# Two routers' position tables in 16 bit, weights copied one stage earlier, and a new order in the rotary products and at the end

## What is computed

```
x = x + ga * causal_attention(h)              # layer 0
x = x + gb * one_of_8_experts(h)              # layer 0: a token goes to its best expert, 320 places each
K = rotary(Xn @ Wk); V = rotary(Xn @ Wv)      # layer 1, the mixer
A = sum over tokens of (K/|K|) * (V/|V|)      # one row of 256
A = 0.5*A + 0.5
x = x + ga * ((A * Q) @ W_out + b_out + h)
out = sum over the 2 best experts e of mult[t,e] * ((silu(h @ w1[e].T) * (h @ w3[e].T)) @ w2[e].T)
x = x + gb * out                              # layer 1: 8 experts, inner width 512
```

## Time and profile before

| | us |
|---|---|
| median of 3 runs | 1075.88 (1074.55 to 1075.96) |
| the profiled execution, its own time | 1077.33 |
| the span of the profile | 1075.6 |
| PE busy | 966.8 (90%) |
| DVE busy | 638.4 (59%) |
| ACT busy | 517.6 (48%) |
| POOL busy | 291.8 (27%) |

### The profile page before, as it was taken

One profiled execution on the slowest core, in us unless ns is written; L12 is line 12 of the kernel. 1 busy time (PEld: TensorE's weight loads), 2 busy tenths in 40 slices (PEclk: granted clock), 3 DMA queues, 4 the chain that ended last, 5 costly groups with the idle time before them and its releaser, 6 DMA issues. The chain is left out here.

```text
span 1075.6 us, 24763 instructions
## 1 busy us (share of the span) xinstructions
PE 966.8 (90%) x9950; PEld 637.2 (59%) x9951; DVE 638.4 (59%) x1683; ACT 517.6 (48%) x809; POOL 291.8 (27%) x347
## 2 busy tenths in 40 slices
PE   6788899999999999997769999978885799999993
PEld 4433334455444444444347777766664799999993
DVE  5568999999889979675710010079677533333331
ACT  3532567767875786663221222246533444444440
POOL 2100320110111011132034434224550255544541
PEclk9978999999999999999869999999997899999997
DMA  5881000000000000000944677330560032233224
GB/s 184 177 175 21 2 2 2 3 3 2 3 3 2 2 3 2 2 4 25 377 139 110 201 223 224 94 91 1 177 215 1 26 57 49 46 49 48 46 43 98
DMA packets 63279, 78.87 MB, mean 73 GB/s; under 512 B 12096, under 2 KB 54976, under 8 KB 62736
## 3 DMA queue, kind: packets, MB, share of 16 engines
q1 hardware_dynamic: 50688, 61.54, 19.0%
q0 software_dynamic: 11968, 15.47, 8.6%
q10 hardware_dynamic: 528, 0.52, 0.1%
HBM read 58.12 MB, written 21.36 MB: 74 GB/s over the span
## 5 line engine op out<-in xcount | busy, mean ns | idle before, releaser
L622 ACT ACTIVATE k_prob<-f_s 128x1024 f32<-128x1024 f32 (+3 forms) x320 | 270.1, 896 | 121.3 <-PE f_s L460 120.6
L682 DVE TENSOR_REDUCE k_mpart<-f_r 128x1 f32<-128x512 f32 x384 | 250.5, 685 | 34.3 <-PE f_r L403 32.0
L403 PE MATMUL f_r<-k_ks,k_qs 112*32 112x512 bf16 (+3 forms) x2560 | 212.7, 357 | 19.7 <-DMA k_qs<-q_dram 7.8
L460 PE MATMUL f_s<-k_qs,k_ks 114*32 114x512 bf16 (+3 forms) x2560 | 175.4, 350 | 1.9 <-ACT k_prob L622 1.3
L882 POOL TENSOR_SCALAR_AFFINE_SELECT k_prob<-k_prob 128x256 f32<-128x256 f32 x128 | 51.3, 407 | 383.9 <-ACT k_prob L622 382.6
L403 PEld LDWEIGHTS f_r<-k_ks,k_qs 112*32 112x32 bf16 x2560 | 71.0, 96 | 136.6 <-DVE k_mpart L682 56.0
L476 PE MATMUL f_o<-k_prob,k_vaug 128*32 128x512 f32 (+3 forms) x1280 | 147.0, 531 | 1.5 <-POOL k_prob L882 1.4
L679 DVE CUSTOM_DVE_ANT_0 k_unread<-f_r,k_causal 128x128 bf16<-128x128 f32 (+3 forms) x256 | 121.1, 484 | 19.2 <-PE f_r L403 18.1
L460 PEld LDWEIGHTS f_s<-k_qs,k_ks 114*32 114x32 bf16 x2560 | 66.1, 97 | 77.7 <-issue 27.6
L2347 DVE TENSOR_TENSOR mid<-silu_g,e_u 128x512 f32<-128x512 f32 x39 | 26.8, 687 | 111.3 <-PE e_u L2248 110.4
L1419 DVE SCALAR_TENSOR_TENSOR outr<-p_o,k_w,k_mod 128x256 f32<-128x256 f32 x16 | 7.7, 484 | 128.2 <-PE p_o L1348 128.2
(11 more groups left out here) (401 smaller groups left out, 1263.4 us busy)
## 6 DMA issues: line engine op xcount, KB each, us to landing
k_w1T<-in_L_ffn_w_dram SPq DMA_DIRECT2D x18, 512.0 KB, 9.7
k_w1T<-in_L_ffn_wi_dram SPq DMA_DIRECT2D x8, 1024.0 KB, 5.9
k_w1T<-in_L_ffn_wo_dram SPq DMA_DIRECT2D x8, 1024.0 KB, 9.5
k_qs<-q_dram SPq DMA_DIRECT2D x6, 768.0 KB, 9.5
h_rows<-k_h SPq DMA_DIRECT2D x8, 512.0 KB, 6.5
sum<-k_x SPq DMA_DIRECT2D x8, 512.0 KB, 6.2
q_dram<-k_room SPq DMA_DIRECT2D x12, 256.0 KB, 8.8
k_rot_t<-in_L_ffn_w_dram SPq DMA_DIRECT2D x6, 512.0 KB, 4.7
```

Of the source, the lines that this page charges most:

```text
L403: last = nc.tensor.matmul(dst[32 * j:32 * (j + 1), :], qs[0:KROWS, c, GH * g + hs, q0:q0 + 32], ks[0:KROWS, QC * ck:QC * ck + w], start=Tr ...
L460: last = nc.tensor.matmul(sc[h % 2][32 * j:32 * (j + 1), i, off:QC], ks[0:KALL, k0:k0 + 32], qs[0:KALL, c, GH * g + 2 * pair + i, off:QC], ...
L622: nc.scalar.activation(prob[:, u % 2, 2 * pair:2 * pair + 2, off:QC], sc[h % 2][:, :, off:QC], ACT.Exp, scale=HD ** -0.5).then_inc(e_done, 1)
L682: nc.vector.reduce_max(mpart[:, s % 2, hs, t, ck:ck + 1], bank(r)[:, 0:w], AX.X).then_inc(ring_used[r % RING], 1)
```

## The change

Five edits. 1: in both routers the constant tables all_pos and hi_of are written as 16-bit values by DVE ahead of the busy part, pos is 16-bit, and at_pos is laid out with the token tile innermost, so that its weights for PE are 128 values that lie 32 bytes apart. 2: in the mixer DVE does the last three tiles' products with the rotary table (rotate), POOL does thirteen. 3: in the mixer gate_rows(2) and add_rows(2) come later in DVE's order. 4: the weights of the first two blocks of layer 1 are copied at the end of router 1, by ACT and DVE, and no longer at the start of the experts. 5: for the last block PE does the second product of the block before ahead of e_u, and DVE's copy_y of that block comes ahead of its last gate.

```diff
+BY_POOL = 13
 # router 0
-pos = sb("pos", [P, NT])
-at_pos, at_blk = sb("at_pos", [P, NT, P], BF), sb("at_blk", [P, NT, NS0], BF)
+pos = sb("pos", [P, NT], BF)
+at_pos, at_blk = sb("at_pos", [P, P, NT], BF), sb("at_blk", [P, NT, NS0], BF)
+all_pos, hi_of = sb("all_pos", [P, P, NT], BF), sb("hi_of", [P, NT, NS0], BF)
-                return nc.tensor.matmul(out, at_pos[:, i, :], code[:, i, c0:c1, :].rearrange("p c b -> p (c b)"),
+                return nc.tensor.matmul(out, at_pos[:, :, i], code[:, i, c0:c1, :].rearrange("p c b -> p (c b)"),
             add_logits(0)
+            nc.vector.tensor_copy(all_pos[:, :, :], last_bcast(iota_pos[:, :], NT))
+            step(nc.vector.tensor_copy(hi_of[:, :, :], last_bcast(iota_hi[:, :], NS0)))
             add_logits(1)
-            step(tt(code[:, :, 1, :], at_blk[:, :, :], last_bcast(iota_hi[:, :], NS0), ALU.mult))
+            step(tt(code[:, :, 1, :], at_blk[:, :, :], hi_of[:, :, :], ALU.mult))
-                tt(at_pos[:, some, :], bcast(iota_pos[:, :], NT // 2), last_bcast(pos[:, some], P),
+                tt(at_pos[:, :, some], all_pos[:, :, some], bcast(pos[:, some], P),
                    ALU.is_equal).then_inc(pos_ready, 1)
 # router 1: pos, all_pos, hi_of, at_pos and k.at_pos in the same way
+all_pos, hi_of = sb("all_pos", [P, BLK, NT], BF), sb("hi_of", [P, 2 * NT, NB], BF)
             step(nc.vector.memset(cont[:, :, 0], 0.0))
+            dve.wait_ge(iota_ready, 7)
+            nc.vector.tensor_copy(hi_of[:, :, :], last_bcast(iota_hi[:, :], NB))
             turned(2)
...
             add_logits(0)
+            step(nc.vector.tensor_copy(all_pos[:, :, :], last_bcast(iota_pos[:, :], NT)))
             add_logits(1)
...
-            step(nc.vector.tensor_copy(k.block_expert[:, :], blk_e[:, :]))
+            nc.vector.tensor_copy(k.block_expert[:, :], blk_e[:, :]).then_inc(blocks_ready, 1)
+            dve.wait_ge(blocks_ready, 1)
...
+            # end of ACT's part
+            act.wait_ge(blocks_ready, 1)
+            for b in range(2):
+                e = act.value_load(k.block_expert[0:1, b:b + 1], min_val=0, max_val=E - 1)
+                nc.scalar.copy(k.wg[:, b, :], k.w1T[:, e, 0, :]).then_inc(k.wg_ready, 1)
+            # end of DVE's part
+            dve.wait_ge(k.w_act, HALVES - BY_DVE0)
+            for b in range(2):
+                e = dve.value_load(k.block_expert[0:1, b:b + 1], min_val=0, max_val=E - 1)
+                nc.vector.tensor_copy(k.wu[:, b, :], k.w1T[:, e, 1, :]).then_inc(k.wu_ready, 1)
 # mixer, SP
-            sp.wait_ge(trig_ready, NT)
+            sp.wait_ge(trig_ready, BY_POOL)
+            sp.wait_ge(rotated, NT - BY_POOL)
             load_raw(sp, k, a, 4)
 # mixer, POOL
             token_weights(2 * TQ, 3 * TQ)
-            turn_products(13)
-            turn_products(14)
             token_weights(3 * TQ, NT - 1)
             token_weights(NT - 1, NT)
-            turn_products(15)
 # mixer, DVE
+            def rotate(i):
+                dve.wait_ge(prod_ready, i + 1)
+                tt(prods[:, i, 2:4, :], prods[:, i, 0::3, :], rot_t[:, i, :, :], ALU.mult).then_inc(rotated, 1)
             for i in range(9, NT):
                 products(i)
-                if i in (9, 11, 13):
+                if i in (9, 11):
                     gate_rows((i - 9) // 2)
                 if i in (10, 12):
                     add_rows((i - 10) // 2)
-            add_rows(2)
+                if i >= BY_POOL:
+                    rotate(i)
+            gate_rows(2)
             dve.wait_ge(A_done, 1)
...
             nc.vector.tensor_copy(bq_rep[:, :, :], last_bcast(bq[:, :], P)).then_inc(wout_ready, 1)
+            add_rows(2)
             dve.wait_ge(A_done, 2)
 # mixer, PE, sum_products(q)
-                pe.wait_ge(trig_ready, TQ * (q + 1))
+                pe.wait_ge(trig_ready, min(TQ * (q + 1), BY_POOL))
+                if q == NC - 1:
+                    pe.wait_ge(rotated, NT - BY_POOL)
 # experts of layer 1, PE, body()
                 product(pg[s], s, wg, g_done)
+                if tail:
+                    second(i - 1, 1, expert_of(b - 1))
                 pe.wait_ge(wu_ready, b + 1)
                 product(pu[s], s, wu, u_done)
...
-                if not head:
+                if not head and not tail:
 # slot_weights (PE)
-                    last = nc.tensor.matmul(pw[:, :, :].rearrange("p n b -> p (n b)"), k.at_pos[:, j, i, :],
+                    last = nc.tensor.matmul(pw[:, :, :].rearrange("p n b -> p (n b)"), k.at_pos[:, j, :, i],
 # ACT
-            gate_weights(0, 0)
             rows(0, 0)
-            gate_weights(0, 1)
 # DVE
-            up_weights(0)
-            up_weights(1)
             rows_of_slots()
...
             for b in range(NB):
+                if b == NB - 1:
+                    copy_y(b - 1)
                 gate(b)
...
-                if b >= 1:
+                if 1 <= b < NB - 1:
                     copy_y(b - 1)
```

More of the change, by code:

```diff
@@ L1482, in phase_router1 @@
         delta_ready, exp_done = sem("r1_delta_ready"), sem("r1_exp_done")
-        code_ready = sem("r1_code_ready")
+        code_ready, blocks_ready = sem("r1_code_ready"), sem("r1_blocks_ready")
         pos_ready = [sem(f"r1_pos_ready{j}") for j in range(2)]
@@ L1553, in _ @@
                 for i in range(NT):
-                    last = nc.tensor.matmul(pinv[:, 0:2 * NB], k.at_pos[:, j, i, :],
+                    last = nc.tensor.matmul(pinv[:, 0:2 * NB], k.at_pos[:, j, :, i],
                                             code_of[:, j, i, :, :].rearrange("p s b -> p (s b)"),
@@ L1662, in _ @@
             step(ts(code_of[:, :, :, 0, :].rearrange(flat4), at_blk[:, :, :, :].rearrange(flat4), tok1[:, 0:1], None, ALU.mult))
-            tt(code_of[:, :, :, 1, :].rearrange(flat4), at_blk[:, :, :, :].rearrange(flat4), last_bcast(iota_hi[:, :], NB),
+            tt(code_of[:, :, :, 1, :].rearrange(flat4), at_blk[:, :, :, :].rearrange(flat4), hi_of[:, :, :],
                ALU.mult).then_inc(code_ready, 1)
             for j in range(2):
-                tt(k.at_pos[:, j, :, :], bcast(iota_pos[:, :], NT), last_bcast(pos[:, NT * j:NT * (j + 1)], BLK),
+                tt(k.at_pos[:, j, :, :], all_pos[:, :, :], bcast(pos[:, NT * j:NT * (j + 1)], BLK),
                    ALU.is_equal).then_inc(pos_ready[j], 1)
@@ L1759, in phase_mix @@
         trig_ready, inv_ready, w_ready = sem("m_trig_ready"), sem("m_inv_ready"), sem("m_w_ready")
-        tok_zero = sem("m_tok_zero")
+        tok_zero, rotated = sem("m_tok_zero"), sem("m_rotated")
         A_done, Arow_ready, A_ready = sem("m_A_done"), sem("m_Arow_ready"), sem("m_A_ready")
@@ L2210, in phase_experts1 @@
         m = ctx.enter_context(nc.sbuf_tensor("mid1", [P, 2, F1], FP))
-        rot = k.rot_t[:, :, :, :].rearrange("p i s n -> p (i s n)")
-        wg = rot[:, 0:2048].rearrange("p (s n) -> p s n", s=2)
-        wu = rot[:, 2048:4096].rearrange("p (s n) -> p s n", s=2)
+        wg, wu = k.wg, k.wu
         y = ctx.enter_context(nc.sbuf_tensor("y1", [P, 2, D], FP))
-        wg_ready = sem("e1_wg_ready")
-        wu_ready = sem("e1_wu_ready")
+        wg_ready, wu_ready = k.wg_ready, k.wu_ready
         t_done = sem("e1_t_done")
@@ L2563, in build @@
         with experts1:
-            k.at_pos = sbuf(experts1, "at_pos", [P, 2, NT, BLK], BF)
+            k.at_pos = sbuf(experts1, "at_pos", [P, 2, BLK, NT], BF)
             k.hT1 = sbuf(experts1, "hT1", [P, 2 * KH * QC])
@@ L2574, in build @@
             k.x_in1 = [sem(f"x_in1_{s}") for s in range(2)]
+            k.wg_ready, k.wu_ready = sem("wg_ready"), sem("wu_ready")
+            rot = k.rot_t[:, :, :, :].rearrange("p i s n -> p (i s n)")
+            k.wg = rot[:, 0:2048].rearrange("p (s n) -> p s n", s=2)
+            k.wu = rot[:, 2048:4096].rearrange("p (s n) -> p s n", s=2)
             if upto >= 8:
```

4 lines of the change are left out of this document (2 added, 2 removed).

## The result

Over the first runs of both kernels the median went from 1075.77 us (7 runs, 1073.33 to 1076.04) to 1063.94 (7 runs, 1062.84 to 1070.38), ratio 0.9923, 95% interval 0.9902 to 0.9944. A later set gave 1067.93 (12 runs, 1063.74 to 1071.72) against 1074.73, ratio 0.9939 (0.9919 to 0.9959). So the change takes 8.3 us by the first ratio (6.0 to 10.5 by its interval) and 6.6 by the second (4.4 to 8.7); the forecast, 1068.1, was 0.9927 of 1075.88. The ratio applied to 1075.88 gives 1067.6, and the median of the 12 later runs is 1067.93; both lie inside the range.

What follows compares the result with a forecast made beforehand. PE bounds layer 1's experts (215.8 of 219 us), DMA is busy throughout around router 0, and gains lie at joints between stretches. 2.8 + 1.0 + 1.0 + 2.1 + 0.9 = 7.8 us, from 1075.88 to 1068.1; range 1066.0 to 1072.3.

Steps and rivals of the forecast that it cites:

- Router 1's tables: DVE's 16-bit products at 0.52 ns per element bring the list, gather and barrier of router 1 2.8 us sooner.
- Router 0's tables: DVE's faster products bring router 0's list and gathers 1.26 us sooner; 1.0 us taken, bounds 0 and 1.26.
- SP is late next and caps the gain near 1.3: Router 0: the gather's landing would come at 544.85, just behind SP's end at 544.76, which limits the gain.
- Rival 3: Router 0's gather stays tied to the loads, or POOL's powers keep PE waiting: 1.0 to 1.5 less, 1069.4; chance 0.12.
- PE's spread weights: Both routers and slot_weights: PE's loads of weights 32 bytes apart cost 0; bounds 0 and 0.08 us per load.
- Rivals 1 and 5: PE's loads slow: first, 5.0 us lost at full price, 1073.1, chance 0.28; second, 0.20 us per load, 1080.9, chance 0.03.
- Weight copies: Start of layer 1's experts: copies hide under router 1's gather landing, xT starts sooner behind PE; 1.0 us.
- The mixer: PE, POOL and DVE meet near 767.3, so PE's last sum starts sooner; 2.1 us, bounds 1.0 and 2.6.
- SP loads 2.3 us earlier, so the wait at 775.88 moves as well: Mixer: SP's load of raw weights over the rotary table, and PE's wait for it, come sooner too.
- Rival 4: Mixer: with PE's 2.22 us wait gone, a stretch at 1.2 GHz may go too; 1066.6, chance 0.08.
- One sign of being wrong: Mixer: the prediction is wrong if a moved DVE pass ends later than PE needs it; no size given.
- The end: Last scatters: each waits for the landing before it, the last two 4.4 us apart; 0.9 us, bounds 0.5 and 1.3.

Runs made afterwards that it cites:

- e11: The kernel after with router 1's copy all_pos moved behind the last add of the logits; one run of 1069.00 us.
- e5: The kernel before with only the position tables' layout changed and two added copies, positions left in float32; ratio 1.0004.
- e1: The kernel before with the 16-bit tables in the new layout alone, in both routers; 1071.89 us, ratio 0.9963.
- e6: The kernel after with four more copies by ACT ahead of the first blocks' weight copies in router 1; 1070.35 us, ratio 0.9948.
- e9: The kernel after with another order in the mixer: PE turns the late raw weights last, DVE's add_rows passes placed anew; 1064.33 us, ratio 0.9905.
- e7: The kernel after without its mixer edits: POOL turns all 16 tiles, DVE's gate_rows and add_rows as before; 1070.60 us, ratio 0.9961.
- e12: The kernel after with one more rotary product moved from POOL to DVE (12 by POOL, 4 by DVE); one run of 1069.47 us.

## Why the prediction was right, and where it was not

- **Size and sign.** 7.8 us forecast; 8.3 and 6.6 by the two ratios. That they lie so near it is in part luck: by stage the terms add up to 6.0 us in the mean, for the reasons below, and each ratio has an interval of more than 4 us.
- **Router 1's tables**, 2.8: measured 2.78 and, alone, 2.80. The products took 1218 and 808 ns where 1230 and 810 were put down; the copy all_pos took 1.23 us in its gap, and 1.29 us more once it stood outside (e11). The rate of 0.52 ns per element was an estimate from the copy's 699 ns for 1024 elements. The runs show it for this product: 1218 ns for 2048 elements with pos in 16 bit, and 2284 (e5) with pos in 32.
- **Router 0's tables**, 1.0 of 1.26: the gather moved 1.25 us in e1 and 1.28 in the kernel after, as priced, PE's start by 0.7 in the mean of the profiles (23.82 to 23.11). The step that said "SP is late next and caps the gain near 1.3" was right, and the profiled pair shows it (24.11 to 22.84). The mean is lower because the profiled execution of the kernel before was the slowest of its six and SP's last issue came late in two of the eight with the tables (e1, e6). Rival 3 has the size, from SP and not from the gather's landing.
- **PE's spread weights**, taken at 0: 54 ns per load, hidden but for 0.27 us in slot_weights. The choice of 0 was nearly right, but not its reason, that "little of it" is "in bare loading": a load took 98 ns in slot_weights and 134 in router 1 even before, more than the 76 ns of a product there, and what hides it is that loads overlap products (the 32 loads of slot_weights, 98 ns each, lie in the 1.89 us of its products). Rivals 1 and 5 fell. The loads did become slower (152 ns for 98 in slot_weights, 162 for 134 in router 1), and it cost 0.3 us of rival 1's 5.0.
- **Weight copies**, 1.0: measured 1.07, under the gather's landing with 1.65 us to spare. I had them done by 831.8, so 1.4 ahead of the landing.
- **The mixer**, 2.1, is the term that was mis-sized. The first half of it was right: rotate took 0.43 us, and the sum ended 2.1 us sooner, like with like (2.55 in the kernel after). What failed is "SP loads 2.3 us earlier, so the wait at 775.88 moves as well". The load did move by 2.6 us in the kernel after, but PE was done with A's products 4.0 us sooner, 2.55 by the sum and 1.4 as its turns now ran at full clock (1.00 against 0.68), so its wait grew from 0.64 to 2 us. Behind it the clock fell in four executions of seven, for 1.6 to 1.7 us, and router 1's logits lost 0.84 us in all eight; the sum had no term for either. The mean over the profiles is 89.25 to 87.80, 1.45 us, less 0.84: 0.6 us. At its best it is 2.5 less 0.84. Rival 4 was right about the stretch at half clock: it went with the wait of 2.22 us in all eight executions with the edits, and PE gained 1.4 us by it. But the gain ended in the wait for the raw weights, and I hadn't asked what the clock would do behind that one. One sign of being wrong also came true without harm: add_rows(2) ended at 763.56 us, 0.5 behind PE's products for A, and held A up by 0.4 us, under the wait for the raw weights.
- **The end**, 0.9: 0.6 and 0.85 in the two executions of the kernel after, 0.80 in the mean. Both scatters are bound by the landing before them, as forecast.
- **Sum of the means**: 2.8 + 0.7 + 1.1 + 0.6 + 0.8 = 6.0 us, against 6.6 and 8.3 by the times. From router 0's begin to the end the profiled executions took 567.94 us before and 558.92 and 559.08 after, 9 us less. Both of these had the mixer at a clock of 0.97, against 0.94, and from layer 0's first expert product to the mixer's begin they took 162.89 and 163.14 us against 164.15. e9, e11 and e6, with the same code there, have 164.1 to 164.4, so I don't count it to the change. One stage is in no row of the table: from e_g to the last scatter but two it is 213.4 to 214.0 us in six executions and 214.8 to 215.2 in eight, with and without each edit, as PE's clock was at 0.5 for 3.0 to 3.9 or for 5.3 to 6.2 us of it. The profiled execution of the kernel before has the shortest, 213.40.
- **Open**: why router 1's logits run at a lower clock whenever the mixer's edits are in, and what decides between the two outcomes behind the 2 us wait. No run here sets the clock. The kernel without the edits was slower by time (1070.60 against 1067.93) while the edits alone gained nothing that the times show. The profiles account for 1.4 of these 2.7 us in the mixer and router 1's logits, and e7 has another 1.1 us from e_g to the last scatter but two (214.98 against 213.93 and 213.85), where its clock stayed low longer; that this comes from the edits is not shown.

## What to carry to other kernels

When you remove a wait, compute the next wait of the same engine with both of its sides moved: here the data moved by 2.6 us and the engine by 4.0, and behind the wait that grew the clock fell in four executions of seven. Look at the clock behind the wait that goes, too: of PE's 4.0 us, 1.4 came from it. Where executions of one kernel differ by more than an edit is worth, read each stage from its own first instruction, over several executions, and take the mean. Price cover by taking it away: four extra copies showed 1.65 us of room, and one copy moved out of its gap showed its full 1.2.

## What the hardware showed that I had not expected

- The stretch ahead of router 0, the same code in every kernel, took 502.45 to 507.74 us in fourteen executions.
- Behind a wait of 1.9 to 2.1 us in the mixer PE ran its next 22 matmuls in 3.36 us at full clock (three executions) or in 5.03 us at a mean clock of 0.66 (four), with the same code of the mixer but for e12's one product. Behind the wait of 2.22 us of the kernel before the clock fell in all six.
- Weights of 128 values 32 bytes apart loaded in 152 ns in place of 98.
- Router 1's end did not wait for ACT when ACT ended 1.35 us behind the gather's start; when it ended 4.26 us behind, the end waited, and PE's next instruction followed ACT's end by 0.30 us.
